# A hybrid layer on one core: attention B's key-score steps in a new order, attention A's causal mask added by VectorE

## The chip, the core and the metric

The kernel runs on one core of a Trainium2 chip, as one program. The metric is the device time of one execution in microseconds. Three runs of the kernel before gave 1072.94, 1072.4 and 1072.7 us, a median of 1072.7. The engines are TensorE (PE, matrix products; PEld is its weight load), VectorE (DVE), ScalarE (ACT), GpSimd (POOL) and SyncE (SP, which issues transfers here). PE writes its results to PSUM, eight banks of 128 partitions x 512 f32; DVE and ACT read and write PSUM, GpSimd doesn't.

## The reference

Four parts, each on the layer norm of a residual x of 2 x 512 x 512 f32: attention A, a mixture of experts, attention B, the same experts again. The two attentions, cut to what matters:

```python
# attention A: 32 heads of 128, 8 key/value heads, weights as 4-bit codes with scales
scores = einsum('bhqd,bhkd->bhqk', rope(q), rope(k)) * scale + mask      # mask: 0, or -inf above the diagonal
out = einsum('bhqk,bhkd->bhqd', softmax(scores), v)
return out @ dequant(o_codes, o_scales)

# attention B: 32 heads of 16, 8 key/value heads
att = where(causal, einsum('bhgqd,bhkd->bhgqk', qg, k) / sqrt(16), -inf)
ctx = einsum('bhgqk,bhkd->bhgqd', softmax(att), v)
return ctx @ Wo
```

## The kernel before

Every f32 product is made of three 16-bit ones (high x high, high x low, low x high), so each result is also split into a high and a low part by ACT and DVE. Waits between engines are semaphores, and each engine runs its own instruction list in order; the order of the work is written out by hand in each engine's block.

**Attention A.** It runs in 8 groups (j), one for each key/value head, and in each group over 8 heads s (four query heads times two batches). Groups 1 to 6 are a hardware loop. For a head, PE's `scores` (L1050) makes four row tiles of 128 queries in the order `A_ORDER = (3, 0, 2, 1)`; tile i has (i + 1) x 128 key columns. Each tile is three products (L1069 to L1071) and a fourth (L1072): identity times the 128x128 mask, added onto the last 128 columns. DVE's `a_max` (L1572) takes the row maximum of each tile out of PSUM (L1579), ACT's `a_exps` (L721) scales the four maxima, then writes the exponentials back into the same PSUM tiles with the row sum as accumulator output (L730). DVE's `row_factors` (L1585, L1588) makes the factors, ACT's `probs_high` (L761) the high part of the probabilities and DVE's `probs_low` (L1595) the low part; SP transposes both by DMA, and PE's `a_pv` (L1090 to L1092) uses them two heads later. Between these, PE makes projections (`project`), which DVE turns by position (`rope`, L1563 to L1565), and output tiles (`a_out`), which DVE adds to x (`o_add`, L1607); `ctx_low` (L1602) is the low part of the context. PE's `scores` of head s waits, before tile 0, for two low parts of head s - 1 (L1064), and before tile 1 for three. A projection or output tile waits until the holder of its bank, four places earlier in a ring of four banks, has been read.

**Attention B.** It runs over 16 sets q (eight key/value heads times two batches) of four heads each. Since the heads have 16 columns, scores are made twice. First, two sets ahead, `b_scores(q, c, i)` makes query-by-key scores of pair c, row tile i, whose row maxima DVE's `b_max` takes (L1909, L1910, L1912). GpSimd's `b_split` (L661 to L669, five small operations) splits the maxima into three 16-bit terms, PE's `b_turn_max` (L1319) transposes them, DVE's `b_max_out` (L1919) copies them out as `m_turned`. Then `b_keys(q, step)`, steps 0 to 4, makes the key-by-query scores (L1326), takes the maxima away (L1331), adds the mask (L1292), and ACT takes ten exponentials of a set from three key banks (L742, L746). `b_pv(quad, kt)`, kt 0 to 3, makes the context (L1383), ACT copies it (L752), `b_ctx_turn` transposes it (L1393), DVE divides it by the sums (`b_ctx`, L1894 and L1896). `B_STEPS` is the list of the score steps and the turned maxima in the order in which PE makes and DVE reads them; step number n uses the bank pair 2 x (n mod 2) and waits until step n - 2 has been read. A key step waits until the exponential two loads back is done, key step 0 also for `m_turned`. One turn of the loop at L1396 makes the key steps of set q, the scores (q+1, 1, 2), (q+1, 1, 1), (q+2, 0, ...) and (q+2, 1, 3), the turned maxima of q+1, the context of q-1 and the context turn of q-2. ACT's list for a turn (L966 to L972) is exponentials 0 to 7, the context copy, exponentials 8 and 9.

Of the kernel before, what the change touches and what calls it, by code (L numbers as in the profile page):

```python
# [44 lines left out]
MASKED = -1e30  # L45

# [61 lines left out]
for _q in range(SETS):  # L108
    B_STEPS += [(_q, 1, 2), (_q, 1, 1)]
    B_STEPS += [(_q + 1, 0, 3), (_q + 1, 0, 2)] if _q + 1 < SETS else []  # L110
    B_STEPS += [(_q, "max", 0)]
    B_STEPS += [(_q + 1, 0, 1), (_q + 1, 1, 3)] if _q + 1 < SETS else []
# [57 lines left out]
def build(nc, t_in, out):  # L170
    ctx = ExitStack()
    with ctx:
# [18 lines left out]
        mask_b = sb("mask_b", [P, P], BF16)  # L191
# [259 lines left out]
        def _(pool):  # L451
# [4 lines left out]
                      allow_small_or_imprecise_dtypes=True).then_inc(consts, 1)  # L456
            pool.wait_ge(consts, 4)
# [221 lines left out]
        def _(act):  # L679
# [286 lines left out]
            for q in range(SETS + 2):  # L966
                if q < SETS:
                    b_exps(q, range(8))
                if 1 <= q <= SETS:
                    b_ctx_out(q - 1)  # L970
                if q < SETS:
                    b_exps(q, range(8, LOADS))  # L972
# [6 lines left out]
        def _(pe):  # L979
# [70 lines left out]
            def scores(j, s, first):  # L1050
# [7 lines left out]
                for i in A_ORDER:  # L1058
# [12 lines left out]
                    pe.matmul(o_ap, q_lo[:, s, qs], k_hi[:, b, 0:w], start=False, stop=False)  # L1071
                    mm = pe.matmul(bank[bk][:, o + w - P:o + w], ident_b[:], mask_b[:], start=False, stop=True)  # L1072
# [323 lines left out]
            for q in range(-1, SETS + 2):  # L1396
                here = 0 <= q < SETS
                ahead = q + 1 < SETS
                ahead2 = q + 2 < SETS
                back = 1 <= q <= SETS  # L1400
                if here:
                    b_keys(q, 0)
                if ahead:
                    b_scores(q + 1, 1, 2)
                if here:
                    b_keys(q, 1)
                if ahead:
                    b_scores(q + 1, 1, 1)
                if q >= 2:
                    b_ctx_turn(q - 2)  # L1410
                if ahead2:
                    b_scores(q + 2, 0, 3)
                if here:
                    b_keys(q, 2)
                if back:
                    b_pv(q - 1, 0)
                if ahead2:
                    b_scores(q + 2, 0, 2)
                if ahead:
                    b_turn_max(q + 1)  # L1420
                if here:
                    b_keys(q, 3)
                if ahead2:
                    b_scores(q + 2, 0, 1)
                if back:
                    for kt in range(1, ST):
                        b_pv(q - 1, kt)
                if here:
                    b_keys(q, 4)
                if ahead2:  # L1430
                    b_scores(q + 2, 1, 3)
# [13 lines left out]
        def _(dve):  # L1445
# [97 lines left out]
            dve.tensor_copy(mask_b[:], mask_f[:]).then_inc(chain, 1)  # L1543
# [28 lines left out]
            def a_max(j, s):  # L1572

                n = 8 * j + s
                for c, i in enumerate(A_ORDER):
                    bk, o = a_bank(i, s)
                    if i != 2:
                        dve.wait_ge(s_ps, 3 * n + {3: 1, 0: 2, 1: 3}[i])
                    dve.tensor_reduce(smax[:, s % 2, c:c + 1], bank[bk][:, o:o + (i + 1) * P], AX,  # L1579
                                      ALU.max).then_inc(smax_done, 1)  # L1580
# [320 lines left out]
            def b_max(q, c, i):  # L1901
# [4 lines left out]
                if i == 3 and c == 0 and q >= 2:  # L1906
# [17 lines left out]
            for q in range(-1, SETS + 2):  # L1924
                ahead = q + 1 < SETS
                ahead2 = q + 2 < SETS
                if ahead:
                    b_max(q + 1, 1, 2)
                    b_max(q + 1, 1, 1)
                if q >= 2:  # L1930
                    b_ctx(q - 2)
                if ahead2:
                    b_max(q + 2, 0, 3)
                    b_max(q + 2, 0, 2)
                if ahead:
                    b_max_out(q + 1)
                if ahead2:
                    b_max(q + 2, 0, 1)
                    b_max(q + 2, 1, 3)
            m_low(NT, 1.0)  # L1940
# [84 lines left out]
```

## Time and profile before

| | |
|---|---|
| three runs, median | 1072.7 us (1072.4 to 1072.94) |
| profiled execution, its own time | 1071.69 us |
| its span (first to last instruction) | 1069.8 us |
| busy in the span: PE, DVE | 977.9 us (91%), 793.5 us (74%) |
| busy in the span: ACT, POOL | 624.7 us (58%), 579.0 us (54%) |
| attention A | about 48 to 697 us |
| attention B, the loop over sets | about 821 to 989 us |
| mean granted TensorE clock | 0.979 of 2.4 GHz |

Times in the profile are microseconds from the first instruction. "Idle before" is the time in which the engine did nothing ahead of an instruction, with what released it. A matmul's duration is modelled and is longer than the time until the next may start: consecutive matmuls are read by their starts. Operations on DVE and ACT overlap a little too, so that a run of four takes less than the sum of the four.

### The profile page before, as it was taken

How to read it: one execution, taken by the hardware profiler on the slowest of the kernel's cores; microseconds unless marked ns; L12 is line 12 of the kernel's file. 1: busy time of each engine (PE TensorE's matmuls, PEld its weight loads, DVE VectorE, ACT ScalarE, POOL GpSimd, SP SyncE). 2: the span in 40 equal slices, each digit the busy share in tenths (PEclk: the TensorE clock that was granted, in tenths of full speed). 3: DMA queues.
4: the chain of work that ended last, by engine and by line, in shares of the span. 5: the costliest groups of instructions: out<-in, count | busy, mean ns of one | idle time of the engine just before them, and what ended most of it. 6: DMA issues, size and time to landing. Idle time of an engine off the chain costs nothing.

```text
span 1069.8 us, 21660 instructions
## 1 busy us (share of the span) xinstructions
PE 977.9 (91%) x7971; PEld 551.0 (52%) x7971; DVE 793.5 (74%) x1613; ACT 624.7 (58%) x1362; POOL 579.0 (54%) x569
## 2 busy tenths in 40 slices
PE   3688999999999999999999999789986888888998
PEld 1344555555555555555555555345554444454554
DVE  6876887887787887787887888577777777773744
ACT  2267765765666765666666755435386666777231
POOL 3767876876776876776876872045653101110111
PEclk9898999999999999999999999899998899999999
DMA  8094364475364575464475455200000000000002
GB/s 288 40 192 128 74 193 131 73 192 134 70 192 129 74 192 132 71 192 129 74 192 129 76 152 154 68 1 1 1 1 2 2 2 3 2 2 2 1 2 79
DMA packets 179897, 95.52 MB, mean 89 GB/s; under 512 B 168032, under 2 KB 168544, under 8 KB 175200
## 3 DMA queue, kind: packets, MB, share of 16 engines
q1 hardware_dynamic: 170016, 49.64, 22.7%
q10 hardware_dynamic: 9792, 44.59, 12.9%
q8 instruction: 69, 1.13, 0.5%
q14 instruction: 20, 0.16, 0.0%
HBM read 50.17 MB, written 2.10 MB: 49 GB/s over the span
## 4 chain that ended last, share of the span: by engine, by line
PE 75%; DVE 9%; POOL 5%; ACT 5%; issue 4%; DMA 1%; SPq 0%; ACTq 0%; POOLq 0%; DVEq 0%
PE bank L982 15%; PE bank L983 15%; PE bank L984 15%; PE bank L1383 4%; PE bank L1069 3%; PE bank L1070 3%; PE bank L1071 3%; PE bank L1090 3%; PE bank L1091 3%; PE bank L1092 3%; PE bank L1326 2%; PE bank L1307 1%; DVE smax_b L1909 1%; PE bank L1331 1%; ACT pt L742 1%
## 5 line engine op out<-in xcount | busy, mean ns | idle before, releaser
L497 POOL TENSOR_TENSOR rt<-rt 128x512 f32<-128x512 f32 x80 | 100.9, 1265 | 151.8 <-DVE rt L1565 151.8
L1595 DVE SCALAR_TENSOR_TENSOR bw_hi<-bank,rden,bw_hi 128x128 f16<-128x128 f32 (+3 forms) x256 | 123.3, 544 | 60.4 <-ACT bw_hi L761 60.4
L730 ACT ACTIVATE bank<-bank,shift,c_score 128x128 f32<-128x128 f32 (+3 forms) x256 | 147.2, 604 | 2.1
L761 ACT ACTIVATE bw_hi<-bank,rden 128x128 f16<-128x128 f32 (+3 forms) x256 | 114.0, 529 | 32.1 <-DVE rden L1588 32.0
L1579 DVE TENSOR_REDUCE smax<-bank 128x1 f32<-128x512 f32 (+3 forms) x256 | 109.2, 481 | 26.4 <-PE bank L1072 25.0
L725 ACT ACTIVATE shift<-smax,c_score 128x4 f32<-128x4 f32 x64 | 19.0, 297 | 153.8 <-DVE smax L1579 153.8
L742 ACT ACTIVATE pt<-bank,c_score_b 128x512 f32<-128x512 f32 x128 | 81.0, 684 | 38.8 <-PE bank L1292 38.8
L982 PE MATMUL bank<-xt,wq_hi 128*128 128x512 f16 x256 | 98.2, 383 | 2.0 <-DVE rt L1565 1.8
L983 PE MATMUL bank<-xt,wq_hi 128*128 128x512 f16 x256 | 98.3, 384 | 0.0
L984 PE MATMUL bank<-xt,wq_lo 128*128 128x512 f16 x256 | 98.0, 383 | 0.0
L982 PE MATMUL bank<-wo_hi,arena 128*128 128x512 f16 x256 | 97.3, 380 | 0.4 <-DVE x L1607 0.4
L983 PE MATMUL bank<-wo_lo,arena 128*128 128x512 f16 x256 | 97.3, 380 | 0.0
L984 PE MATMUL bank<-wo_hi,arena 128*128 128x512 f16 x256 | 97.3, 380 | 0.0
L504 POOL TENSOR_TENSOR arena<-rt,arena 128x512 f16<-128x512 f32 x80 | 92.2, 1156 | 5.7 <-ACT arena L714 5.7
L1069 PE MATMUL bank<-arena 128*128 128x512 f16 (+3 forms) x256 | 77.7, 304 | 15.5 <-DVE bw_hi L1595 7.8
L1563 DVE TENSOR_TENSOR rt<-bank,sin_a 64x512 f32<-64x512 f32 x80 | 55.5, 693 | 42.9 <-PE bank L984 42.0
L1090 PE MATMUL bank<-bw_lo,arena 128*128 128x512 f16 (+3 forms) x256 | 77.2, 302 | 7.0 <-DMA bw_lo<-bw_hi 7.0
L1912 DVE TENSOR_REDUCE smax_b<-bank 128x2 f32<-128x1024 f32 x64 | 60.9, 954 | 23.3 <-PE bank L1292 22.4
L1071 PE MATMUL bank<-arena 128*128 128x512 f16 (+3 forms) x256 | 78.0, 305 | 0.0
L1070 PE MATMUL bank<-arena 128*128 128x512 f16 (+3 forms) x256 | 77.9, 304 | 0.0
L1091 PE MATMUL bank<-bw_lo,arena 128*128 128x512 f16 (+3 forms) x256 | 77.3, 302 | 0.0
L661 POOL TENSOR_TENSOR m_stack<-smax_b,one 128x16 bf16<-128x16 f32 x16 | 3.7, 232 | 134.2 <-DVE smax_b L1912 134.2
(234 smaller groups left out, 2728.6 us busy)
## 6 DMA issues: line engine op xcount, KB each, us to landing
qcode<-in_q_codes ACTq DMA_DIRECT2D x8, 1024.0 KB, 5.0
qscale<-in_q_scales ACTq DMA_DIRECT2D x8, 1024.0 KB, 7.9
ocode<-in_o_codes ACTq DMA_DIRECT2D x7, 1024.0 KB, 5.0
oscale<-in_o_scales ACTq DMA_DIRECT2D x7, 1024.0 KB, 8.4
kvcode<-in_k_codes ACTq DMA_DIRECT2D x8, 256.0 KB, 8.0
kvcode<-in_v_codes ACTq DMA_DIRECT2D x8, 256.0 KB, 8.4
kvscale<-in_k_scales ACTq DMA_DIRECT2D x8, 256.0 KB, 8.5
kvscale<-in_v_scales ACTq DMA_DIRECT2D x8, 256.0 KB, 9.0
```

The source lines that it names most:

```text
L730: act.activation(a_rows(i, s), a_rows(i, s), ACT.Exp, bias=shift[:, s % 2, c:c + 1], scale=c_score[:, 0:1], accum_out=bank[3][:, SUMS_AT + ...
L761: act.activation(p_row[:, s % 2, HI_AT[i]:HI_AT[i] + P_STEP * i + 1:P_STEP], turned_back(i, s), ACT.Copy, scale=rden[:, s % 2, c:c + 1]).t ...
L982: pe.matmul(out_ap, a_hi, b_hi, start=(k == 0), stop=False)
L983: pe.matmul(out_ap, a_hi, b_lo, start=False, stop=False)
L984: return pe.matmul(out_ap, a_lo, b_hi, start=False, stop=(stop and k == n - 1))
L1069: pe.matmul(o_ap, q_hi[:, s, qs], k_hi[:, b, 0:w], start=True, stop=False)
L1070: pe.matmul(o_ap, q_hi[:, s, qs], k_lo[:, b, 0:w], start=False, stop=False)
L1071: pe.matmul(o_ap, q_lo[:, s, qs], k_hi[:, b, 0:w], start=False, stop=False)
L1090: pe.matmul(o_ap, v_hi[:, b, vs], hi, start=(kt == 0), stop=False)
L1091: pe.matmul(o_ap, v_hi[:, b, vs], lo, start=False, stop=False)
L1579: dve.tensor_reduce(smax[:, s % 2, c:c + 1], bank[bk][:, o:o + (i + 1) * P], AX, ALU.max).then_inc(smax_done, 1)
L1595: dve.scalar_tensor_tensor(out=p_row[:, s % 2, LO_AT[i]:LO_AT[i] + P_STEP * i + 1:P_STEP], in0=turned_back(i, s), scalar=rden[:, s % 2, c: ...
```

## The change

Two independent edits.

In attention A the mask product of PE (L1072) is gone: the third product of a tile closes it. The row maximum (L1579) becomes one operation that adds, over the whole tile, a mask of up to 512 columns in SBUF (zeros, and the 128x128 mask in its last columns) onto the scores, writes the masked scores back to PSUM and gives their maximum as accumulator output. A nop stands ahead of it.

In attention B the same steps stand in another order in PE's loop, in DVE's loop and in `B_STEPS`, and ACT takes exponential 8 before the context copy. PE's new turn: scores (q+1,1,2); key step 0; context turn of q-2; scores (q+2,0,2), (q+2,0,3); key step 1; context 0; key step 2; scores (q+1,1,1); context 1; key step 3; scores (q+2,0,1), (q+2,1,3); context 2; key step 4; turned maxima of q+1; context 3.

```diff
--- before.py
+++ after.py
@@ -43,6 +43,7 @@
 PROJ_DN_B = 2.0 ** -15
 P_UP = 2.0 ** 15
 MASKED = -1e30
+LOWEST = -3e38
 
 
 TRI = 10 * P
@@ -106,10 +107,11 @@
 SETS = 2 * KV_HEADS
 B_STEPS = [(0, 0, 3), (0, 0, 2), (0, 0, 1), (0, 1, 3)]
 for _q in range(SETS):
-    B_STEPS += [(_q, 1, 2), (_q, 1, 1)]
-    B_STEPS += [(_q + 1, 0, 3), (_q + 1, 0, 2)] if _q + 1 < SETS else []
+    B_STEPS += [(_q, 1, 2)]
+    B_STEPS += [(_q + 1, 0, 2), (_q + 1, 0, 3)] if _q + 1 < SETS else []
+    B_STEPS += [(_q, 1, 1)]
+    B_STEPS += [(_q + 1, 0, 1), (_q + 1, 1, 3)] if _q + 1 < SETS else []
     B_STEPS += [(_q, "max", 0)]
-    B_STEPS += [(_q + 1, 0, 1), (_q + 1, 1, 3)] if _q + 1 < SETS else []
 STEP_AT = {step: i for i, step in enumerate(B_STEPS)}
 KEY_BANKS = (4, 6, 7)
 
@@ -188,7 +190,8 @@
         ident_h = sb("ident_h", [P, P], F16)
         ident_b = sb("ident_b", [P, P], BF16)
         mask_f = sb("mask_f", [P, P], F32)
-        mask_b = sb("mask_b", [P, P], BF16)
+        mask_w = sb("mask_w", [P, S], BF16)
+        mask_b = mask_w[:, S - P:S]
         cos_b = sb("cos_b", [P, ST, B_HD // 2], F32)
         sin_b = sb("sin_b", [P, ST, 2, B_HD // 2], F32)
         iota_e = sb("iota_e", [P, EXPERTS], F32)
@@ -454,6 +457,7 @@
             pool.memset(ones_q[:], 1.0).then_inc(consts, 1)
             pool.iota(iota_e[:], pattern=[[1, EXPERTS]], base=0, channel_multiplier=0,
                       allow_small_or_imprecise_dtypes=True).then_inc(consts, 1)
+            pool.memset(mask_w[:, 0:S - P], 0.0).then_inc(consts, 1)
             pool.wait_ge(consts, 4)
 
             def ln_rsqrt(c, t):
@@ -965,11 +969,11 @@
 
             for q in range(SETS + 2):
                 if q < SETS:
-                    b_exps(q, range(8))
+                    b_exps(q, range(LOADS - 1))
                 if 1 <= q <= SETS:
                     b_ctx_out(q - 1)
                 if q < SETS:
-                    b_exps(q, range(8, LOADS))
+                    b_exps(q, range(LOADS - 1, LOADS))
             for t in range(NT):
                 m_high(NT + t, 1.0)
             experts(1)
@@ -1068,8 +1072,7 @@
                     qs = slice(i * P, (i + 1) * P)
                     pe.matmul(o_ap, q_hi[:, s, qs], k_hi[:, b, 0:w], start=True, stop=False)
                     pe.matmul(o_ap, q_hi[:, s, qs], k_lo[:, b, 0:w], start=False, stop=False)
-                    pe.matmul(o_ap, q_lo[:, s, qs], k_hi[:, b, 0:w], start=False, stop=False)
-                    mm = pe.matmul(bank[bk][:, o + w - P:o + w], ident_b[:], mask_b[:], start=False, stop=True)
+                    mm = pe.matmul(o_ap, q_lo[:, s, qs], k_hi[:, b, 0:w], start=False, stop=True)
                     if i != 0:
                         mm.then_inc(s_ps, 1)
 
@@ -1398,37 +1401,38 @@
                 ahead = q + 1 < SETS
                 ahead2 = q + 2 < SETS
                 back = 1 <= q <= SETS
-                if here:
-                    b_keys(q, 0)
                 if ahead:
                     b_scores(q + 1, 1, 2)
                 if here:
-                    b_keys(q, 1)
-                if ahead:
-                    b_scores(q + 1, 1, 1)
+                    b_keys(q, 0)
                 if q >= 2:
                     b_ctx_turn(q - 2)
                 if ahead2:
+                    b_scores(q + 2, 0, 2)
                     b_scores(q + 2, 0, 3)
                 if here:
-                    b_keys(q, 2)
+                    b_keys(q, 1)
                 if back:
                     b_pv(q - 1, 0)
-                if ahead2:
-                    b_scores(q + 2, 0, 2)
+                if here:
+                    b_keys(q, 2)
                 if ahead:
-                    b_turn_max(q + 1)
+                    b_scores(q + 1, 1, 1)
+                if back:
+                    b_pv(q - 1, 1)
                 if here:
                     b_keys(q, 3)
                 if ahead2:
                     b_scores(q + 2, 0, 1)
+                    b_scores(q + 2, 1, 3)
                 if back:
-                    for kt in range(1, ST):
-                        b_pv(q - 1, kt)
+                    b_pv(q - 1, 2)
                 if here:
                     b_keys(q, 4)
-                if ahead2:
-                    b_scores(q + 2, 1, 3)
+                if ahead:
+                    b_turn_max(q + 1)
+                if back:
+                    b_pv(q - 1, 3)
 
             turn(NT, ctx_b[:, 0], bctx, 2 * KV_HEADS - 1)
             for t in range(NT):
@@ -1540,7 +1544,7 @@
             for t in range(ST, ST + 2):
                 ln_norm(0, t)
             dve.wait_ge(d_const, 16 * N_CONST)
-            dve.tensor_copy(mask_b[:], mask_f[:]).then_inc(chain, 1)
+            dve.tensor_copy(mask_b, mask_f[:]).then_inc(chain, 1)
             dve.tensor_tensor(c_score[:, 0:1], pow_q[:, 0:1], pow_q[:, 1:2], ALU.mult).then_inc(chain, 1)
             dve.tensor_tensor(c_out[:], pow_q[:, 2:3], pow_q[:, 3:4], ALU.mult).then_inc(chain, 1)
             dve.wait_ge(chain, 5)
@@ -1576,8 +1580,10 @@
                     bk, o = a_bank(i, s)
                     if i != 2:
                         dve.wait_ge(s_ps, 3 * n + {3: 1, 0: 2, 1: 3}[i])
-                    dve.tensor_reduce(smax[:, s % 2, c:c + 1], bank[bk][:, o:o + (i + 1) * P], AX,
-                                      ALU.max).then_inc(smax_done, 1)
+                    dve.nop(nofuse=True)
+                    dve.tensor_tensor_reduce(bank[bk][:, o:o + (i + 1) * P], bank[bk][:, o:o + (i + 1) * P],
+                                             mask_w[:, S - (i + 1) * P:S], 1.0, LOWEST, ALU.add, ALU.max,
+                                             smax[:, s % 2, c:c + 1]).then_inc(smax_done, 1)
 
             def row_factors(j, s):
                 n = 8 * j + s
@@ -1903,7 +1909,7 @@
                 at = STEP_AT[q, c, i]
                 two = banks[:, 2 * (at % 2):2 * (at % 2) + 2]
                 dve.wait_ge(bs_ps, at + 1)
-                if i == 3 and c == 0 and q >= 2:
+                if i == 2 and c == 0 and q >= 2:
                     dve.wait_ge(bsplit_done, q - 1)
                 if i == 2:
                     dve.tensor_reduce(smax_b[:, q % 2, c, :, 2], two[:, :, P:4 * P], AX, ALU.max)
@@ -1926,17 +1932,18 @@
                 ahead2 = q + 2 < SETS
                 if ahead:
                     b_max(q + 1, 1, 2)
-                    b_max(q + 1, 1, 1)
                 if q >= 2:
                     b_ctx(q - 2)
                 if ahead2:
+                    b_max(q + 2, 0, 2)
                     b_max(q + 2, 0, 3)
-                    b_max(q + 2, 0, 2)
                 if ahead:
-                    b_max_out(q + 1)
+                    b_max(q + 1, 1, 1)
                 if ahead2:
                     b_max(q + 2, 0, 1)
                     b_max(q + 2, 1, 3)
+                if ahead:
+                    b_max_out(q + 1)
             m_low(NT, 1.0)
             y_adds(NT, 1.0, c_out_b, 3)
             experts(1, None)
```

## Rows read from the trace of the kernel before

**Rows 1.** Busy time by stretch: stretch, length, PE, PEld, DVE, ACT, POOL, clock, DMA.

```profile
285.00:446.00 161.00, 159.91 (x1073) 90.06 (x1074) 125.61 (x257) 103.84 (x257) 119.89 (x102) 1.00 0.56 131
...
655.00:690.00 35.00, 25.67 (x184) 14.86 (x182) 26.35 (x61) 16.46 (x45) 5.62 (x7) 0.96 0.55 149
...
850.00:900.00 50.00, 42.68 (x764) 24.57 (x764) 37.66 (x56) 35.26 (x57) 5.85 (x25) 1.00 0.01 2
```

**Rows 2.** Timeline, attention A, PE: start, us, instruction, [idle before <-releaser].

```profile
293.89 0.38 PE L1069 MATMUL bank<-arena 128*128 128x512 f16 x1
...
299.96 0.22 PE L982 MATMUL bank<-wkv_hi,xt 128*128 128x128 f16 x1
...
302.64 0.38 PE L1069 MATMUL bank<-arena 128*128 128x512 f16 x1
...
303.29 0.22 PE L1072 MATMUL bank<-mask_b,ident_b 128*128 128x128 bf16 x1
...
313.89 0.38 PE L1069 MATMUL bank<-arena 128*128 128x512 f16 x1
```

**Rows 3.** The same, DVE: work of one head.

```profile
295.77 1.67 DVE L1579 TENSOR_REDUCE smax<-bank 128x1 f32<-128x512 f32 x4
...
298.62 0.69 DVE L1563 TENSOR_TENSOR rt<-bank,sin_a 64x512 f32<-64x512 f32 x1 [0.52 <-PE bank L984]
...
300.63 0.15 DVE L1585 TENSOR_SCALAR rsum<-bank 128x4 f32<-128x4 f32 x1
...
301.90 1.93 DVE L1595 SCALAR_TENSOR_TENSOR bw_hi<-bank,rden,bw_hi 128x128 f16<-128x128 f32 x4 [0.91 <-ACT bw_hi L761]
...
304.34 1.67 DVE L1579 TENSOR_REDUCE smax<-bank 128x1 f32<-128x512 f32 x4
```

**Rows 4.** The same, ACT: copies without, exponentials with an accumulator output.

```profile
282.76 1.78 ACT L761 ACTIVATE bw_hi<-bank,rden 128x128 f16<-128x128 f32 x4 [0.27 <-DVE rden L1588]
...
288.77 0.43 ACT L730 ACTIVATE bank<-bank,shift,c_score 128x128 f32<-128x128 f32 x1
...
290.94 0.18 ACT L730 ACTIVATION_READ_ACCUMULATOR bank<-bank,shift,c_score 128x1 f32 x1
...
299.99 0.18 ACT L730 ACTIVATION_READ_ACCUMULATOR bank<-bank,shift,c_score 128x1 f32 x1
```

**Rows 5.** The same, DVE: three small operations at the stage's end.

```profile
678.54 0.18 DVE L1464 BATCH_NORM_AGGREGATE mv<-bn 128x2 f32<-128x6 f32 x1
678.76 0.15 DVE L1466 TENSOR_SCALAR mv<-mv 128x1 f32<-128x1 f32 x1
678.83 0.74 DVE L1607 SCALAR_TENSOR_TENSOR x<-bank,c_out,x 128x512 f32<-128x512 f32 x1
```

**Rows 6.** Timeline, attention B, PE: one turn of the loop.

```profile
901.33 0.34 PE L1326 MATMUL bank<-qt_b,kt_b 64*128 64x384 f16 x2 [0.45 <-ACT pt L742]
...
906.54 0.28 PE L1307 MATMUL bank<-kt_b,qt_b 64*128 64x256 f16 x2 [0.40 <-DVE smax_b L1910]
...
906.81 1.50 PE L1383 MATMUL bank<-pt,bv 128*32 128x384 f32 x24
908.24 0.28 PE L1326 MATMUL bank<-qt_b,kt_b 64*128 64x256 f16 x2
...
909.75 0.39 PE L1326 MATMUL bank<-qt_b,kt_b 64*128 64x512 f16 x2 [0.51 <-ACT pt L746]
...
911.20 0.34 PE L1326 MATMUL bank<-qt_b,kt_b 64*128 64x384 f16 x2 [0.45 <-ACT pt L742]
```

**Rows 7.** The same turn: the split on POOL, and ACT's and DVE's longest idle.

```profile
903.04 0.23 POOL L661 TENSOR_TENSOR m_stack<-smax_b,one 128x16 bf16<-128x16 f32 x1 [8.39 <-DVE smax_b L1912]
...
904.30 0.23 POOL L669 TENSOR_TENSOR m_stack<-low_b,one 128x16 bf16<-128x16 f32 x1
...
906.18 1.27 ACT L742 ACTIVATE pt<-bank,c_score_b 128x512 f32<-128x512 f32 x2 [1.19 <-PE bank L1292]
...
909.29 1.23 DVE L1912 TENSOR_REDUCE smax_b<-bank 128x2 f32<-128x1024 f32 x1 [1.61 <-PE bank L1292]
```

## The prediction

> **What bounds the kernel now.** I read first the busy time by stretch, then the waits inside each stage, since the change touches two stages that have different limits. In attention A the stretch of two head groups from 285 to 446 us has PE busy 159.91 of 161 us at full clock, DVE 125.61 [rows 1]: PE sets the time, DVE has about a fifth of it free. At the end of that stage PE is busy only 25.67 of 35 us, and the chain runs through DVE and ACT [rows 1]. In attention B PE is busy 42.68 of 50 us, DVE 37.66, ACT 35.26 [rows 1]: no engine is full, so waits between them set the time, and the timeline of one turn of its loop has to be read. One turn takes 911.20 - 901.33 = 9.87 us [rows 6], and there are 16 of them.
>
> **Attention A, removed from PE.** Each score tile loses the mask product. One stands at 303.29; what a 128-column product takes is read from 48 of them in a row, 299.96 to 302.64, 0.0558 us each [rows 2]. There are 256 mask products; in the 7 groups after the first PE is full, so 7 x 32 x 0.0558 = 12.5 us can go, of which 0.7 us lie in the last group's last three heads, which PE does not bound. In the first group PE waits for others and I count nothing.
>
> **Attention A, added to DVE.** The row maximum of a tile becomes an add of the mask with a maximum as accumulator output, written back to PSUM, behind a nop that takes the wait. Call the extra time of one such operation over the reduction d; there are four in a head, 256 in all. No row shows the new operation, so I bound its parts. Main part: the four reductions of a head take 1.67 us for 1280 columns, the four scalar-tensor-tensor operations over the same columns, also with two inputs and an output of full width, 1.93 us [rows 3]: 0.065 more each; the low bound is 0, as the stream may run like the reduction. Accumulator output: ACT's exponentials with one take 288.77 to 291.12 (290.94 + 0.18) = 2.35 us, four ACT copies over the same columns without one 1.78 us [rows 4], 0.14 each. On DVE an independent one-column operation delays the next by 0.07 (678.76 to 678.83) [rows 5]. So 0.07 to 0.14. The nop: nothing while DVE is behind its semaphores (low bound), about 0.05 as a guess between nothing and the 0.07 of the tiny operation, both ends kept. The sum goes from 0.07 to 0.28; I take the main part by its nearest row and the read between its two rows, 0.065 + 0.105 = 0.17, the nop hidden.
>
> The Trainium skill (VectorE: DVE Perf Modes, "Two Vector instructions with no wait between them") states that an operation that also writes out its accumulator is two instructions. No DVE row here shows it; the ACT rows show the same form.
>
> **What this does to PE.** PE's block for one head runs from one score step to the next: 302.64 - 293.89 = 8.75 us for head 1 and 313.89 - 302.64 = 11.25 for head 2 [rows 2]. By composition of such blocks (scores 1.86, a projection 2.59, the context product 1.63, an output tile 2.59, the value projection 2.68) heads 0 to 7 of a group are 8.7, 8.75, 11.25, 11.3, 11.3, 8.7, 11.25 and 8.7 us, 79.9 in all. DVE for head 1 runs 295.77 to 304.34, of which 0.52 is a wait for the projection: 8.05 us, in it the wait for ACT's first high part ahead of 301.90 [rows 3]. With the operations of the other heads the eight are about 7.4, 8.05, 10.1, 8.05, 8.7, 8.65, 9.5 and 9.4, 69.8 in all. With d = 0.17 each gets 0.68 more, 75.2, against 78.1 for PE: in sum still under PE. But heads 5, 7, 0 and 1 are heads where DVE now falls behind: 9.3 against 8.45, 10.1 against 8.45, 8.1 against 8.4, 8.7 against 8.5. What waits behind it is the next head's scores: they wait for the low parts of the probabilities of the head before. The room is small: the exponentials end 0.45 us before the row factors start (299.99 + 0.18 against 300.63), and the second low part, about 0.9 us behind 301.90, ends some 0.5 us before the small score tile that follows the mask product of 303.29 [rows 2 to 4]. So about 0.95 us may be lost and the maximum alone takes 0.68 of it. Carried from head to head over a group (a maximum starts at the later of its scores and DVE's last work; row factors at the later of rotation and exponentials; scores at the later of PE and the second low part), a group takes 78.8 us for d = 0.10, 79.5 for 0.17, 80.1 for 0.20, 82.1 for 0.30, 87.3 for 0.50, against 79.85 before, which this carrying also gives. For d = 0.17: 6.5 full groups x -0.35 = -2. At the end of the stage DVE is on the chain with two maxima and PE isn't: 2 x 0.68 = +1.4. In the first group, where PE isn't full, +0.6 (bounds 0 and 8 x 0.68 = 5.4). Attention A in sum: 0, with -7 at d = 0.07 and +15 at d = 0.28.
>
> **Attention B.** Nothing is added or removed, only the order changes. PE waits three times in a turn: 0.45 us (901.33) and 0.51 us (909.75) for an ACT exponential, since the steps for keys 4, 0 and 1 stand close together, and 0.40 us (906.54) for DVE's maxima, since the score steps (0,2), turned maxima and (0,1) stand close together [rows 6]. Ends of matmuls are modelled, so an idle of 0.45 is about 0.6 by starts; in sum 1.36 us shown, about 1.85 by starts. ACT idles 1.19 us before 906.18 and DVE 1.61 us before 909.29 [rows 7], while PE runs the 24 context products of 1.43 us in a block (906.81 to 908.24) [rows 6].
> The new order puts one context product or one group of scores between any two key steps. I placed a turn anew with the old lengths: a key step 0.50 or 0.57 us, two exponentials 1.27 [rows 7], a maximum of a pair of full tiles 1.23 with 1.61 us of idle to spend [rows 7], the split on GpSimd 1.5 us (903.04 to 904.53) [rows 7]. Then each key step finds its bank read; the split has about 2.5 us between the (1,1) scores and the turned maxima; and what stands last are the copy of the turned maxima before key step 0 (0.06 us of wait) and the score banks (0.3 us in two places). That gives 8.3 us a turn. The same placing gives 9.97 for the old order, 0.1 too much. The upper bound is PE's shown busy share, 42.68/50 x 9.87 = 8.43 [rows 1, 6]; one wait of the old size left in makes it 8.8. So 1.1 to 1.7 us in each of 15 turns, minus 1 to 2 us at the start, where the first turned maxima now stand behind 1.8 us more of DVE's work and the split hides under it; the last turns have no scores and change little. 15 x 1.55 - 2 = -21, between -14 and -26.
>
> The value to start from is 1072.7 us, the median; the profiled execution is 1071.69 with a span of 1069.8, so what is taken from its rows counts one to one. 1072.7 - 21 + 0 = 1052.
>
> **The rivals.**
> 1. The new DVE operation is cheap. For it: DVE's small operations overlap well [rows 5]. Against: the two-input operations already pay 0.065 more [rows 3]. With d = 0.07 attention A gives 7 us: 1045. The Trainium skill (Vector Engine (DVE) Microarchitecture Reference, "Measured stream behaviour on trn2") gives about 75 ns an instruction after overlap for one- and two-source and multi-step programs alike, which for one more instruction would be this rival; the four reductions agree with it (1.67 us less 1.333 of stream, 0.084 each), the scalar-tensor-tensor rows don't. Chance 0.15.
> 2. Slower: DVE becomes attention A's bound. The place is heads 5 to 1 of each group, the price beyond the point where the room is used is up to 32 d a group: 82.1 us a group at d = 0.30 (+14 in 6.5 groups, +4 at both ends), 87.3 at 0.50 (+49 and +6). From d of about 0.33 it eats all of attention B's 21 us; at d = 0.50 the time is 1107. For it: a read that has to wait until the pipe is empty, as the 0.22 us between dependent small DVE operations (678.54 to 678.76) would suggest [rows 5], plus a nop that isn't hidden. Against: both ends of my rows stay at or under 0.28. Chance 0.13.
> 3. The same with d from 0.23 to 0.32, so attention B's gain is partly given back: 1058 to 1070. Chance 0.15.
> 4. Attention B's waits change their place: key step 0 waits for split, turned maxima and the copy behind all of DVE's maxima, and the context turn for ACT's copy, which now stands behind exponential 8. If 0.8 us of a turn stays: 15 x 0.8 = 12 us, 1061. DVE's work in a turn (37.66/50 x 9.87 = 7.4 us) leaves only 0.9 us free at 8.3 [rows 1, 6]. Chance 0.10.
> 5. The order doesn't help at all (ACT and PE still alternate): 1072 to 1074. Against it is that ACT needs only 35.26/50 x 9.87 = 7.0 us of a turn [rows 1, 6]. Chance 0.03.
>
> **How the numbers follow.** The forecast (1046 to 1058) has 0.44. A measurement of this kernel tells about 0.2%, 2.1 us, from no change. Faster: forecast, rivals 1, 3 and 4, 0.84. Same: most of rival 5, 0.03. Slower: rival 2, 0.13. The range reaches from inside rival 1 (1043) to the upper end of rival 3 (1069), and leaves rivals 2 and 5 and the far end of 1 outside.
>
> **What would show it.** Right: turns in attention B of 8.2 to 8.5 us, PE busy there above 95%, none of the three waits; in attention A groups of 79 to 80 us, PE with small waits at the score products behind DVE's low parts in heads 7, 0 and 1, and four maxima in about 2.3 us. Wrong: four maxima in more than 3 us and PE busy below 95% between 285 and 446 us (rival 2); key step 0 or the context turn waiting over 0.5 us each turn (rival 4).

## The result

The changed kernel takes 1043.62 us (four runs, 1041.95 to 1046.15) against 1072.55 (1069.7 to 1072.94): a ratio of 0.9738, 95% interval 0.9711 to 0.9765, so 28 us or 2.6% less. A second set of runs beside other kernels gave 0.9728 (0.9703 to 0.9752). The prediction was 1052, with a range of 1043 to 1069. One of the four runs of attention B's edit alone (below) was a slow one, 1294.39 us at a granted clock of 0.75, and is left out there.

The head of the profile's page, with busy time and share; then the group that answers to the row maximum (busy, mean ns, idle before):

```profile
span 1042.5 us, 21597 instructions
...
PE 965.8 (93%) x7715; PEld 533.3 (51%) x7715; DVE 804.2 (77%) x1869; ACT 620.6 (60%) x1362; POOL 580.4 (56%) x570
...
L1584 DVE CUSTOM_DVE_ANT_0 bank<-bank,mask_w 128x512 f32<-128x512 f32 (+3 forms) x256 | 118.1, 520 | 21.6 <-PE bank L1075 21.3
```

PE has the 256 mask products less, 7715 instead of 7971 instructions; DVE has 256 accumulator reads more and 11 us more of busy time.

Three stretches, read from the starts of instructions in the two traces, tell where the time went (us):

| stretch | before | after | difference |
|---|---|---|---|
| first instruction to attention B's first row maximum | 821.53 | 809.84 | -11.7 |
| from there to the end of its loop (first transposes of the output product) | 168.65 | 153.03 | -15.6 |
| the rest | 79.62 | 79.63 | 0 |

In the first stretch, groups 1 to 6 of attention A (from one group's first score product to the next's) take 78.56 us in the mean against 80.18: 6 x 1.62 = 9.7 us. Another 2.0 us are in group 0 (83.93, now 81.92); that group took 80.8 to 85.7 us in the other traces, 83.5 with attention A's edit undone and 80.8 with it alone, so those 2 us aren't surely the change's. The second stretch took 150.54 us in another execution of the changed kernel and 150.56 with attention B's edit alone, so the order is worth 18.1 us there; the 2.5 us between are the clock's, as the part on the ends of attention B shows.

The timeline of PE in attention A. The first row and the fourth are the first score products of groups 1 and 2; the rows between lie in head 1 of group 1, the last two in head 1 of group 2:

```profile
122.40 0.38 PE L1073 MATMUL bank<-arena 128*128 128x512 f16 x1
...
131.27 0.38 PE L1075 MATMUL bank<-arena 128*128 128x512 f16 x1
131.72 0.23 PE L1073 MATMUL bank<-arena 128*128 128x128 f16 x1
...
200.70 0.38 PE L1073 MATMUL bank<-arena 128*128 128x512 f16 x1
...
209.57 0.38 PE L1075 MATMUL bank<-arena 128*128 128x512 f16 x1
210.12 0.23 PE L1073 MATMUL bank<-arena 128*128 128x128 f16 x1 [0.16 <-DVE bw_hi L1601]
```

A group of 78.30 us, 1.55 less than the 79.85 of before; the full price of its 32 mask products is 1.78. The missing 0.23 us lies at 131.72: this product starts 0.45 us behind the one before it, where 0.22 is usual. The small score tile of head 1 waits there for the low parts of head 0, as the last row names it for group 2, where the wait is 0.33 us. It is one of the places where the prediction expected DVE to show. Groups 3 and 5, which follow a head of PE's own loop (it holds two groups a turn, and PE starts 0.8 to 0.9 us late at its head), have no such wait and take 78.07 us, the full 1.78 less. The same stretch as in [rows 1], and one of equal length in attention B (columns as there):

```profile
285.00:446.00 161.00, 160.06 (x1031) 88.26 (x1030) 130.60 (x328) 106.47 (x266) 121.71 (x102) 1.00 0.53 131
...
840.00:890.00 50.00, 50.00 (x912) 27.78 (x908) 43.72 (x66) 40.55 (x66) 7.07 (x30) 1.00 0.01 3
```

PE is still full in attention A, with DVE 5 us busier than in [rows 1]; in attention B it went from 42.68 to 50.00 of 50 us. Now the timeline of DVE, answering to [rows 3], from one head's first maximum to the operation behind its last:

```profile
290.21 0.69 DVE L1584 CUSTOM_DVE_ANT_0 bank<-bank,mask_w 128x512 f32<-128x512 f32 x1
290.81 0.14 DVE L1584 DVE_READ_ACCUMULATOR2_ANT smax<- 128x1 f32 x1
290.81 0.33 DVE L1584 CUSTOM_DVE_ANT_0 bank<-bank,mask_w 128x128 f32<-128x128 f32 x1
...
291.96 0.14 DVE L1584 DVE_READ_ACCUMULATOR2_ANT smax<- 128x1 f32 x1
291.96 0.75 DVE L1613 SCALAR_TENSOR_TENSOR x<-bank,c_out,x 128x512 f32<-128x512 f32 x1
```

The read of the accumulator (DVE_READ_ACCUMULATOR2_ANT) and the next operation start together. Four masked maxima hold DVE from 290.21 to 291.96, 1.75 us; the four reductions of before held it 1.59, from 304.34 [rows 3] to the start of this operation:

```profile
305.93 0.68 DVE L1569 SCALAR_TENSOR_TENSOR arena<-bank,arena 128x512 f16<-128x512 f32 x1
```

So the extra cost d is 0.04 us, not 0.17. The nops have no rows of their own and no gap is left for them.

The chain of waits of attention B, two of its pieces (start, us, what), one turn apart:

```profile
867.34 1.00 PE bank L1386 x8
...
875.73 1.00 PE bank L1386 x8
```

A turn takes 8.39 us instead of 9.87. None of the three waits of PE in [rows 6] is left.

### The profile page after: what moved, and what is told of

It is laid out like the page before. It is cut to its first block, busy times and chain, and to the rows that moved or that the text cites. A ratio compares the mean times of both kernels' runs of the same rounds, so it can differ in the third digit from the quotient of the medians.

```text
span 1042.5 us, 21597 instructions
## 1 busy us (share of the span) xinstructions
PE 965.8 (93%) x7715; PEld 533.3 (51%) x7715; DVE 804.2 (77%) x1869; ACT 620.6 (60%) x1362; POOL 580.4 (56%) x570
## 4 chain that ended last, share of the span: by engine, by line
PE 74%; DVE 9%; POOL 5%; ACT 5%; issue 5%; DMA 1%; SPq 0%; ACTq 0%; DVEq 0%; POOLq 0%
PE bank L986 14%; PE bank L987 14%; PE bank L988 14%; PE bank L1386 4%; PE bank L1073 3%; PE bank L1075 3%; PE bank L1074 3%; PE bank L1093 3%; PE bank L1095 3%; PE bank L1094 3%; PE bank L1329 2%; PE bank L1310 2%; PE bank L1334 2%; PE bank L1295 1%; DVE bank L1584 1%
## 5 line engine op out<-in xcount | busy, mean ns | idle before, releaser
L1584 DVE CUSTOM_DVE_ANT_0 bank<-bank,mask_w 128x512 f32<-128x512 f32 (+3 forms) x256 | 118.1, 520 | 21.6 <-PE bank L1075 21.3
L1073 PE MATMUL bank<-arena 128*128 128x512 f16 (+3 forms) x256 | 74.4, 303 | 16.3 <-DVE bw_hi L1601 8.8
L1093 PE MATMUL bank<-bw_lo,arena 128*128 128x512 f16 (+3 forms) x256 | 77.2, 302 | 7.5 <-DMA bw_lo<-bw_hi 7.1
L1074 PE MATMUL bank<-arena 128*128 128x512 f16 (+3 forms) x256 | 77.7, 303 | 0.0
L1094 PE MATMUL bank<-bw_lo,arena 128*128 128x512 f16 (+3 forms) x256 | 77.3, 302 | 0.0
L1075 PE MATMUL bank<-arena 128*128 128x512 f16 (+3 forms) x256 | 74.9, 304 | 0.0
L1095 PE MATMUL bank<-bw_lo,arena 128*128 128x512 f16 (+3 forms) x256 | 74.0, 302 | 0.0
L1918 DVE TENSOR_REDUCE smax_b<-bank 128x2 f32<-128x1024 f32 (+1 forms) x64 | 58.8, 954 | 17.6 <-PE bank L1295 17.4
```

The lines of the kernel that those rows point to most:

```text
L1073: pe.matmul(o_ap, q_hi[:, s, qs], k_hi[:, b, 0:w], start=True, stop=False)
L1074: pe.matmul(o_ap, q_hi[:, s, qs], k_lo[:, b, 0:w], start=False, stop=False)
L1075: mm = pe.matmul(o_ap, q_lo[:, s, qs], k_hi[:, b, 0:w], start=False, stop=True)
L1093: pe.matmul(o_ap, v_hi[:, b, vs], hi, start=(kt == 0), stop=False)
L1094: pe.matmul(o_ap, v_hi[:, b, vs], lo, start=False, stop=False)
L1584: dve.tensor_tensor_reduce(bank[bk][:, o:o + (i + 1) * P], bank[bk][:, o:o + (i + 1) * P], mask_w[:, S - (i + 1) * P:S], 1.0, LOWEST, ALU. ...
```

## The experiments

All are compared with the kernel before on the same chip, as the ratio of the times with its 95% interval. The first four split the change.

**Attention A's edit alone.** The changed kernel with `B_STEPS` and the loops of PE, DVE and ACT in attention B as before.

> Attention A's edit alone, attention B in the order of before. By the two traces attention A ends 11.8 us earlier after the change, and the two parts should not touch each other: 1072.5 - 12 = 1060.5 us (1059 to 1062). If attention A's part had stayed near zero, as I predicted, and the rest came from attention B: 1072.

Measured: 0.9906 (0.9889 to 0.9922), 10.1 us less, 1061.55 us; turns of 9.87 us. That is 1 us more than expected and inside the 1059 to 1062 that I gave.

**Attention B's edit alone.**

> Attention B's order alone, with the mask product and the plain row maximum of before in attention A. By the traces the loop over the sets and its end give 15.5 us net: 1072.5 - 15.5 = 1057 us (1055 to 1059), turns of 8.4 us. By my prediction of 21 us: 1051.5.

Measured: 0.9834 (0.9814 to 0.9854), 17.8 us less, 1054.99 us; turns of 8.39 us. 0.9906 x 0.9834 = 0.9742, the whole change's 0.9738: the two parts don't touch each other.

**The DVE part of attention A alone.**

```diff
 # the new row maximum, and still:
+                    mm = pe.matmul(bank[bk][:, o + w - P:o + w], ident_b[:], mask_b, start=False, stop=True)
```

> Attention A's new row maximum on DVE, but PE still makes the mask product (the mask is added twice, which changes no probability); attention B as before. It prices the DVE part alone. If it costs 0.04 us an operation (traces): groups of 79.9 to 80.0 us and about +1 us in all, 1072 to 1075. If it costs my 0.17: groups of about 81 us and +8 to +10 us.

Measured: 0.9992 (0.998 to 1.0005), nothing. The groups are those of before (79.85 and, ahead of a head of PE's loop, 81.0). My 0.17 would have shown.

**The PE part alone.**

```diff
-                    mm = pe.matmul(bank[bk][:, o + w - P:o + w], ident_b[:], mask_b[:], start=False, stop=True)
```

> The mask product is left out and nothing replaces it, so attention A is computed without the causal mask; the row maximum and attention B are those of before. It prices PE's part alone. 224 products of 0.0558 us lie in groups where PE is full, and the first group also gained 2 us in the trace: 1072.5 - 14 = 1058.5 us (1057 to 1060). If the first group's gain came from elsewhere: 1060.5.

Measured: 0.9874 (0.9857 to 0.989), 13.5 us less; groups 78.07 us, all of the 1.78 us. Together the single parts make 13.5 + 0.9 = 14.4 us less, the edit itself 10.1: an operation that cost nothing while PE was slower seems to cost 3 to 4 us once PE is quicker. The intervals leave 1 to 7 us for this, and the traces show less of it: groups 1 to 6 take 78.64 us in the mean with the whole edit and 78.50 with PE's part alone, 0.8 us in six groups, which is the waits at head 1. The rest, if there is any, would lie at the ends of the stage and isn't resolved.

**How much DVE work attention A bears.** d was far from my estimate, so these two test the next step, from d to the time. One or two reductions more in each head:

```diff
                                              smax[:, s % 2, c:c + 1]).then_inc(smax_done, 1)
+                    if c == 0:
+                        for e in range(1):                      # second kernel: range(2)
+                            dve.tensor_reduce(pad_m[:, e:e + 1], x[:, 0], AX, ALU.max)
```

> The changed kernel with one more DVE reduction (512 columns in SBUF, about 0.6 us) behind the first of a head's four row maxima, which makes the extra cost of an operation as if d = 0.04 + 0.15 = 0.19 us. It tests the step from d to the time. By my carrying of lag from head to head: groups of 79.9 us instead of 78.3, 6.5 x 1.6 + about 2 at both ends = +12, 1044 + 12 = 1056 us. If DVE's fifth of idle hides it: +2 us, 1046.

> The same with two such reductions, as if d = 0.34 us: the place where my slower rival was to decide. By the carrying: groups of 83 us, 6.5 x 4.7 + about 4 = +35, 1079 us, slower than before the change. If only the sum of DVE's work over a group counted (69.8 + 32 x 0.34 = 80.8 us a group): +20, 1064.

Measured with one: 0.9862 (0.9837 to 0.9887), 1057.43 us, 14 to 15 us over the changed kernel. With two: 1.0242 (1.0216 to 1.0268), 1097.2 us, 26 us slower than before the change and 18 more than expected.

The carrying knows nothing of what happens at the head of a loop, so it has to be held against group 1, the only one ahead of all loop heads: 79.94 us with one reduction and 82.78 with two, where I had 79.9 and 83. There the first reduction costs 1.6 us a group over the 78.30 of the changed kernel, the second 2.8. Over groups 1 to 6 the means are 78.56, 79.88 and 85.28 us, so here the second costs 5.4, more than the 4.8 us of its own work (0.60 us in each of eight heads). With one reduction the sum, near the 12 of the carrying, is partly luck: groups 1 to 6 give 6 x 1.3 = 8 us and the ends of the stage 6 to 7, where I had 10 and 2.

What makes the rest in the kernel with two reductions begins at the head of DVE's loop, the start of group 2. First its first row maximum there, then the same place in the changed kernel:

```profile
215.38 0.70 DVE L1585 CUSTOM_DVE_ANT_0 bank<-bank,mask_w 128x512 f32<-128x512 f32 x1 [2.02 <-issue]
```

```profile
202.50 0.74 DVE L1613 SCALAR_TENSOR_TENSOR x<-bank,c_out,x 128x512 f32<-128x512 f32 x1
203.16 0.69 DVE L1584 CUSTOM_DVE_ANT_0 bank<-bank,mask_w 128x512 f32<-128x512 f32 x1
```

With two reductions DVE stands for 2.02 us though its data is there ("issue"), and for 1.99 to 2.03 us at the start of each of groups 3 to 6 as well. In the changed kernel, in the kernel before (206.22 and 206.88) and in the one with one reduction (206.80 and 207.46) the maximum follows the last operation of the group before without a gap, so there is no gap that idle time could hide. What is different is how often instructions are loaded. These are the rows of queue q14 (transfers, MB, share) in the pages of the changed kernel, of the kernel with one reduction and of the one with two:

```profile
q14 instruction: 21, 0.17, 0.1%
...
q14 instruction: 21, 0.17, 0.1%
...
q14 instruction: 47, 0.39, 0.1%
```

Of the 47, 26 fall between 210 and 640 us, in groups 2 to 6, where the other two kernels have one, and two fall between 211 and 213.5 us, about the start of the gap of 213.36 to 215.38. This suggests that the second reduction makes DVE's list too long to stay loaded, so that each turn of the loop fetches it again. That is argued and not shown: no run separates it from the lag. So the kernel with two reductions measures more than the work that was added.

What follows from the gap: PE's score products of the next head, then busy time and clock (last but two columns) in the wait and behind it.

```profile
218.91 0.38 PE L1074 MATMUL bank<-arena 128*128 128x512 f16 x1
...
223.49 0.29 PE L1074 MATMUL bank<-arena 128*128 128x128 f16 x1 [3.77 <-DVE bw_hi L1605]
...
225.38 0.63 PE L987 MATMUL bank<-xt,wq_hi 128*128 128x512 f16 x1
225.80 0.63 PE L988 MATMUL bank<-xt,wq_hi 128*128 128x512 f16 x1
```

```profile
219.60:223.40 3.80, 0.12 (x1) 0.00 (x0) 2.12 (x7) 3.79 (x12) 2.77 (x3) 0.80 0.14 19
223.40:229.40 6.00, 5.92 (x20) 2.71 (x21) 5.24 (x15) 1.88 (x7) 3.21 (x3) 0.56 0.92 349
```

The gap comes on top of the lag, PE waits 3.77 us in the next head, and behind the wait the mean granted clock is 0.56, most of the stretch at the 1.2 GHz level: a 512-column product takes 0.42 us (225.38 to 225.80) instead of 0.216. My carrying had neither the gap nor the clock.

**ACT's list in attention B.** The edit there is one exponential moved over the context copy. First the changed kernel without it, then this move alone, in the kernel with attention A's edit:

```diff
-                    b_exps(q, range(LOADS - 1))
+                    b_exps(q, range(8))
...
-                    b_exps(q, range(LOADS - 1, LOADS))
+                    b_exps(q, range(8, LOADS))
```

> The changed kernel with ACT's list of before: exponentials 0 to 7, the context copy, 8 and 9. The copy waits for context product 3, which PE makes behind key step 4 and the turned maxima, so ACT idles 0.5 to 0.6 us there and exponentials 8, 9, 0 and 1 come later. If this reaches PE (the rival in which waits change their place): turns of 8.6 to 8.9 us, +3 to +8 us. If ACT's idle share hides it: turns of 8.39, no change.

> Attention A's edit, and of attention B's edit only ACT's list (exponentials 0 to 8, the context copy, 9), with PE's and DVE's order of before. In the old order context product 3 stands ahead of key step 4, so the copy there has nothing to wait for, and the context turn stands 2 us later. If ACT's list is good only together with PE's new order: turns of 9.87 us or a little more, 1061 to 1064 us. If ACT's list is what frees the turn whatever PE does: turns of 9 us or less, 1048.

Measured without it: 0.9852 (0.9834 to 0.987), 1056.04 us, and turns of 9.38 us. With it alone: 0.9949 (0.9932 to 0.9967), 1066.34 us, turns of 10.06. Both came out outside what I had written, the first by twice.

| turn of attention B, us | ACT's list of before | ACT's new list |
|---|---|---|
| PE's and DVE's order of before | 9.87 | 10.06 |
| PE's and DVE's new order | 9.38 | 8.39 |

ACT's timeline in the changed kernel, where the copy (L756) stands between exponentials 8 and 9:

```profile
872.25 0.69 ACT L750 ACTIVATE pt<-bank,c_score_b 128x512 f32<-128x512 f32 x1 [0.40 <-PE bank L1295]
872.96 0.60 ACT L756 ACTIVATE ctx_t<-bank 128x512 f32<-128x512 f32 x1
873.46 0.68 ACT L750 ACTIVATE pt<-bank,c_score_b 128x512 f32<-128x512 f32 x1
```

The same place without the move, on ACT and then on PE, which here makes key step 0 of the next set:

```profile
875.63 0.60 ACT L756 ACTIVATE ctx_t<-bank 128x512 f32<-128x512 f32 x1 [1.11 <-PE bank L1386]
876.12 1.26 ACT L750 ACTIVATE pt<-bank,c_score_b 128x512 f32<-128x512 f32 x2
```

```profile
876.86 0.39 PE L1329 MATMUL bank<-qt_b,kt_b 64*128 64x512 f16 x2 [0.85 <-ACT pt L750]
```

The new PE order puts context product 3 last in the turn. With the old list ACT waits 1.11 us for it with exponential 8 behind, and PE's next key step waits 0.85 us for that exponential. In the new list exponential 8 runs in ACT's wait. With PE's old order the move is a loss, since product 3 is ready early and the copy filled ACT's wait for key step 4. There exponential 8 now waits 1.57 us with the copy behind it, so the exponentials after the copy come later, and a key step of PE waits 0.65 us for one of them where it waited 0.45 [rows 6]. The context turn has no wait. ACT, then PE:

```profile
900.01 0.69 ACT L749 ACTIVATE pt<-bank,c_score_b 128x512 f32<-128x512 f32 x1 [1.57 <-PE bank L1294]
900.60 0.59 ACT L755 ACTIVATE ctx_t<-bank 128x512 f32<-128x512 f32 x1
```

```profile
902.40 0.34 PE L1328 MATMUL bank<-qt_b,kt_b 64*128 64x384 f16 x2 [0.65 <-ACT pt L745]
```

**The ends of attention B.** Here the first trace of the changed kernel seemed to show two losses. From the loop's first maximum to the first context product took 22.9 us before, 23.9 after. And the last two intervals between the first context products of neighbouring sets took 8.53 and 5.34 us before, now 8.01 and 7.42. An order of the ends meant to win both back:

```diff
-for _q in range(SETS):
+B_STEPS += [(0, 1, 2), (0, 1, 1), (1, 0, 3), (1, 0, 2), (0, "max", 0), (1, 0, 1), (1, 1, 3)]
+for _q in range(1, SETS):
 # PE, last turn with key steps (q = SETS - 1):
+                if q == SETS - 1:
+                    b_pv(q - 1, 2)
+                    b_pv(q - 1, 3)
                 if here:
                     b_keys(q, 3)
+                if q == SETS - 1:
+                    b_ctx_turn(q - 1)
                 if here:
                     b_keys(q, 4)
 # ACT, same turn: exponentials 0 to 5, the copy, 6 to 9
```

> The changed kernel with attention B's two ends in another order: at the start the turned maxima of set 0 stand before the scores (1,0,1) and (1,1,3), as before the change; in the last turn with key steps the context of the set before is finished ahead of key step 3, ACT copies it after exponential 5, and its context turn stands ahead of key step 4. By the traces the start cost 1.0 us and the end 2.1 us, and in one execution the clock fell to 0.62 in the last context products for 1.3 us more: 3 to 4 us faster than the changed kernel, 1040 us. If these waits only move to ACT's exponentials: 1043.

> The changed kernel as it is, on the same chip beside the three others: 1044 us, 1042 to 1046. In its profile I look at whether the clock falls in the last context products again.

Measured: the reordered ends 0.9721 (0.9698 to 0.9744), the changed kernel beside them 0.9728 (0.9703 to 0.9752): no difference.

The loss at the start is not the order's. The same stretch, from the loop's first maximum to the first context product, in the first execution of the changed kernel, in its second and in the kernel before (columns as in [rows 1]):

```profile
809.84:833.70 23.86, 17.59 (x248) 10.21 (x246) 20.08 (x28) 9.96 (x16) 2.35 (x10) 0.60 0.00 1
...
812.50:835.19 22.69, 16.20 (x248) 9.57 (x247) 20.06 (x28) 9.96 (x16) 2.35 (x10) 0.66 0.00 1
...
821.53:844.42 22.89, 17.39 (x251) 10.07 (x249) 20.24 (x28) 11.22 (x18) 2.65 (x12) 0.66 0.01 1
```

At the same granted clock of 0.66 the new order is 0.2 us quicker here; the 1.0 us appears only where the clock was 0.60. Attention B's edit alone and the changed kernel with ACT's list of before take 22.7 us too. In the three executions with the reordered ends the stretch took 21.65 us at 0.71, 23.59 at 0.60 and 24.16 at 0.55: it follows the clock, and what the other order of the start is worth can't be told from them.

At the end, the wait for the context of set 14 is gone, but the last context products now wait for the exponentials, and the interval is 6.72 us instead of 7.42. There too the clock differs between executions. The last 32 context products in the reordered kernel, then in the changed one in the second set of runs:

```profile
954.72 4.05 PE L1388 MATMUL bank<-pt,bv 128*32 128x512 f32 x32 [1.45 <-ACT pt L751]
```

```profile
959.46 2.36 PE L1386 MATMUL bank<-pt,bv 128*32 128x512 f32 x32 [0.81 <-DVE ctx_b L1902]
```

The first had a granted clock of 0.50 from 955 to 958 us, the second 1.00. In the first set's execution of the changed kernel these 32 took 3.69 us at a mean of 0.62, 1.3 us more. To see whether the idle ahead of them brings the clock down, six unused products fill it:

```diff
+                if q == SETS - 1:
+                    for _ in range(6):
+                        pe.matmul(bank[1], ident_b[:], m_turned[:, q % 2], start=True, stop=True)
```

> The kernel with attention B's ends reordered, and six unused products of 128x512 (6 x 0.213 = 1.28 us) on PE behind key step 4 of the last set, where PE waited 1.5 us for the exponentials and the granted clock then stood at 0.50 in the last context products. If the idle brought the clock down: the last 32 context products take 2.4 us instead of some 4.7, and the time is 2 us under the reordered kernel. If the clock falls for another reason: no change, or up to 0.2 us more.

> The reordered ends once more, on the same chip as the one with the unused products: 1041 to 1042 us; in the profile the clock of the last context products shows whether the fall comes in each execution.

With the fill PE is busy 1.29 of the 1.5 us ahead of the products and the clock is 1.00. But without it, in this set's execution, PE was busy 0.05 of 1.5 us and the clock was 1.00 too:

```profile
959.85 2.36 PE L1388 MATMUL bank<-pt,bv 128*32 128x512 f32 x32 [1.45 <-ACT pt L751]
```

The times are 0.9714 (0.9698 to 0.973) with the fill and 0.9737 (0.9724 to 0.975) without. The intervals overlap, and the profile shows no difference in mechanism; whether the fill is worth anything stays open. No version was shown to beat the changed kernel.

## Why the prediction came out as it did

The sign and attention B's mechanism were right. The time, 1043.62 us, lies only 0.6 us inside the lower end of the range and outside the forecast of 1046 to 1058: what came was nearest to rival 1 (1045, chance 0.15). Of the signs that were to show it right, the turns (8.39 us) and PE's share in attention B held; the groups (78.07 to 79.33 us) are mostly under the 79 to 80 named, and four maxima take 1.75 us instead of 2.3. The size was made of two errors that partly cancel: attention A 0 forecast and -10.1 us measured, attention B -21 and -17.8.

**The price of the new DVE operation (wrong).** The step that failed is the term d: 0.17 us forecast, 0.04 measured, under even the low end of 0.07. Both of its parts were too high. The main part was priced by the scalar-tensor-tensor rows [rows 3], 0.065 over the reduction; the new operation shows 0.04 together with all the rest. The accumulator read was priced between ACT's 0.14 and the 0.07 of a small DVE operation [rows 4, 5]; on DVE it starts together with the next operation and delays nothing that the trace shows. Rival 1 had it, at d = 0.07 and with a chance of 0.15; the low bound should have been zero for the read too, since no row excluded that. By the rule of the Trainium skill cited there (Vector Engine (DVE) Microarchitecture Reference, "Measured stream behaviour on trn2") a read counted as one more instruction would by estimate have cost about 0.075 us, so the trace goes below it as well.

**From d to the time (right, up to a point).** The carrying has 78.8 us a group at d = 0.10, and PE's own blocks are 78.1, so at d = 0.04 it lies between them; inside PE's loop body 78.30 and 78.07 were measured. The wait came in one head of eight, head 1, behind head 0's low parts; the prediction had named three. With one and two added reductions group 1 took 79.94 and 82.78 us where the carrying has 79.9 and 83. It failed behind the loop's head with two: the gap of 2.0 us and the lower clock were missing. The slower rival's place was right in the main (with two reductions PE waits at heads 0 and 1 most). Its price can't be judged by the 26 us at d = 0.34, where I had the point of no gain at 0.33, since five gaps of 2.0 us and what they set off are in it.

**The PE term (right).** 12.5 us less 0.7 forecast; the PE part alone gave 13.5 with an interval of about 1.8 either way.

**Attention B's turn (right).** 8.3 us forecast, 8.39 measured, 50.00 of 50 us busy. Something like rival 4, waits that change their place, is what happens without the moved exponential (9.38 us), though key step 0 then waits for exponential 8 and not for the turned maxima. I had put that move down as part of the order and given it no price; with the new order it carries 1.0 of the 1.48 us a turn.

**The number of turns and the ends (wrong).** I counted 15 full turns. The trace has 13 intervals of 9.87 us, now 8.39 or slightly less (8.16 in the last): 13 x 1.48 + 0.2 = 19.5 us. The next gains 0.5, the last loses 2.1, and the start gains 0.2, which makes 18.1. That is what the second execution and attention B's edit alone show. In the first execution the lower clock takes 1.2 of it at the start and 1.3 at the end, and 15.6 are left. Three terms were mis-sized: 15 turns instead of 13 (3 us too much), 1 to 2 us of loss at the start that no run shows (2 too little), and "the last turns change little", where 1.6 us are lost. That the first two nearly cancel is luck. The new order makes context product 3 of set 14 the last of its turn, so the context of set 14 is copied, turned and divided between the last exponentials and the last context products with nothing beside it:

```profile
956.52 0.66 PE L1396 MATMUL bank<-ident,ctx_t 128*128 128x128 f32 x4 [0.91 <-ACT ctx_t L756]
957.99 3.69 PE L1386 MATMUL bank<-pt,bv 128*32 128x512 f32 x32 [0.81 <-DVE ctx_b L1902]
```

## What to carry to other kernels

Moving small work from a full engine to one with a fifth of idle pays, but the idle isn't one pool: carry the lag through the few units in which the receiving engine is behind, since the first 0.6 us a head cost 1.6 us a group here and the next 0.6 cost 2.8, where nothing else disturbed. A test that adds instructions to a loop can change more than the work: look at the instruction transfers before you read its price (here 47 against 21, and 5.4 us a group instead of 2.8). When the order of one engine's list changes, move the entries of its partners' lists with it: here one exponential on ACT was worth two thirds of the gain of the whole new order, and was a loss without it. Count the steady turns in the trace and price the first and the last ones by themselves, from stretches with the same granted clock.

## What the runs showed of the hardware

- A DVE operation with an accumulator output has a read of its own in the trace (0.14 us), which starts together with the next operation: four masked maxima with reads 1.75 us, four reductions 1.59. On ACT an accumulator output cost 0.14 each, by the comparison of exponentials with copies [rows 4].
- At the head of a hardware loop DVE stood for 1.99 to 2.03 us in the one kernel that loaded instructions on q14 47 times, and not at all in the kernels with 20 or 21. In the kernels before and after PE started 0.8 to 1.0 us late at the head of its loop.
- After waits of PE of 0.8 to 3.8 us the granted clock had a mean of 0.50 to 0.62 in some executions, and stayed at 1.00 in others of the same kernel with the same waits (0.9 and 0.8 us: 0.62 and 1.00; 1.45 us: 0.50 and 1.00). What decides it was not found. The start of attention B took 22.69 us at a mean clock of 0.66 and 23.86 at 0.60, with the same instructions.
